# One of every 128 gathers of the first layer moved from GpSimd to SyncE, as one-row transfers

## The reference, cut to what matters

```python
def _L0_gnn_ref(node_features, edge_features, edge_index, We1, be1, We2, be2, Wn1, bn1, Wn2, bn2):
    src_f = node_features[src]
    dst_f = node_features[dst]
    edge_in = jnp.concatenate([src_f, dst_f, edge_features], axis=1)
    h = jax.nn.relu(edge_in @ We1 + be1)
    edge_msg = jax.nn.relu(h @ We2 + be2)
    node_in = jnp.concatenate([dst_f, edge_msg], axis=1)
    h2 = jax.nn.relu(node_in @ Wn1 + bn1)
    node_msg = jax.nn.relu(h2 @ Wn2 + bn2)
    agg = jax.ops.segment_sum(node_msg, dst, num_segments=node_features.shape[0])
    return node_features + agg

h = jnp.maximum(_layernorm(x, axis=-1), 0.0)
x = x + _L0_gnn_ref(h, edge_attr_64, edge_index, ...)
h = jnp.maximum(_layernorm(x, axis=-1), 0.0)
x = x + _L1_gnn_ref(h, src, dst, edge_type_8, edge_weight1, ...)   # H[etype, src] summed over dst
```

## Time and profile before

| what | value |
|---|---|
| median of three runs | 11777.57 us |
| the profiled execution, its own time | 11662.24 us |
| its span in the profile | 11659.8 us |
| PE busy | 7838.2 us, 67% |
| POOL busy | 5846.3 us, 50% |
| DVE busy | 4276.2 us, 37% |
| ACT busy | 2363.0 us, 20% |
| POOL L617 from `p_tab` (first layer) | 3128 gathers, 943 ns each |
| mean granted TensorE clock | 0.78 of full speed |

### The profile page before, as it was taken

How to read it: one execution, slowest core, us unless ns; L and a number is a source line. 1 busy time by engine, 2 the same in 40 slices (tenths; PEclk the granted TensorE clock), 3 DMA queues, 4 the chain that set the end, 5 groups by cost and what they waited for, 6 DMA issues and landing times.

```text
span 11659.8 us, 215368 instructions
## 1 busy us (share of the span) xinstructions
PE 7838.2 (67%) x52954; PEld 6037.6 (52%) x52954; DVE 4276.2 (37%) x15012; ACT 2363.0 (20%) x7307; POOL 5846.3 (50%) x6213
## 2 busy tenths in 40 slices
PE   6777777777777777776555655655565555655555
PEld 5655566565665566565444444444444444444444
DVE  4333333333333333334333333333333333333333
ACT  4333333333333333334000000000000000000000
POOL 3555555555555555554444444444444444444444
PEclk8888888888888888888776777767767776777777
DMA  4222222222222222222111111111111111111111
GB/s 105 64 64 63 63 64 63 63 64 64 63 64 64 63 63 64 62 64 76 35 34 34 35 35 35 36 35 34 35 35 34 35 35 34 36 35 35 35 35 52
DMA packets 630303, 585.31 MB, mean 50 GB/s; under 512 B 306227, under 2 KB 505147, under 8 KB 629228
## 3 DMA queue, kind: packets, MB, share of 16 engines
q0 software_dynamic: 197856, 251.86, 9.9%
q1 hardware_dynamic: 422268, 325.27, 9.7%
q10 hardware_dynamic: 9600, 1.60, 0.1%
HBM read 558.88 MB, written 19.27 MB: 50 GB/s over the span
## 4 chain that ended last, share of the span: by engine, by line
SPq 31%; issue 21%; DVE 0%; PE 0%; DMA 0%; ACT 0%; DVEq 0%
SPq L548 26%; SPq L543 4%; SPq L448 1%; SPq L538 0%; SPq L555 0%; DVE res L1057 0%; SPq L414 0%; SPq L354 0%; PE bank L1222 0%; PE bank L1209 0%; DMA h_tab<-h_place 0%; PE bank L1255 0%; SPq L564 0%; DMA h_place<-in_src_t 0%; ACT h_place L660 0%
## 5 line engine op out<-in xcount | busy, mean ns | idle before, releaser
L617 POOL DMA_INDIRECT rows_place<-h_tab,idx x3055 | 2881.8, 943 | 3237.7 <-DMA idx<-in_src_t 1871.4
L617 POOL DMA_INDIRECT shared<-p_tab,idx x3128 | 2950.0, 943 | 2472.7 <-remote 992.1
L1209 PE MATMUL bank<-shared,rows_place 128*128 128x256 f32 x6110 | 2155.8, 508 | 902.4 <-DMA rows_place<-h_tab,idx 609.7
L1021 DVE SCALAR_TENSOR_TENSOR shared<-bank,key,late 128x256 f32<-128x256 f32 x3128 | 1280.3, 476 | 2932.8 <-remote 1843.2
L1209 PEld LDWEIGHTS bank<-shared,rows_place 128*128 128x128 f32 x6110 | 1490.7, 255 | 1286.0 <-DMA rows_place<-h_tab,idx 629.1
L1115 PE MATMUL bank<-h_sb,w_tile 128*128 128x128 f32 x6256 | 1079.3, 325 | 892.8 <-DVE h_sb L932 874.4
L1115 PEld LDWEIGHTS bank<-h_sb,w_tile 128*128 128x128 f32 x6256 | 909.8, 224 | 1105.0 <-DVE h_sb L932 1095.1
L775 ACT ACTIVATE h_place<-bank 128x256 f32<-128x256 f32 x782 | 298.7, 383 | 5773.2 <-remote 3342.2
L1222 PE MATMUL bank<-h_place,w_rel_sb 128*128 128x64 f32 x6256 | 915.2, 297 | 332.1 <-issue 331.4
L1134 PE MATMUL bank<-wn_half,h_sb 128*128 128x128 f32 x6256 | 1078.3, 326 | 0.0
L1222 PEld LDWEIGHTS bank<-h_place,w_rel_sb 128*128 128x128 f32 x6256 | 844.1, 212 | 348.6 <-issue 323.3
(11 more groups left out here) (94 smaller groups left out, 7034.4 us busy)
## 6 DMA issues: line engine op xcount, KB each, us to landing
rows_place<-in_dst_c SPq DMA_DIRECT2D x782, 192.0 KB
h_place<-h_tab SPq DMA_DIRECT2D x6272, 0.5 KB
shared<-in_edge_cols SPq DMA_DIRECT2D x782, 128.0 KB
shared<-p_tab,idx POOLq DMA_INDIRECT x3128
h_place<-h_tab ACTq DMA_DIRECT2D x3072, 0.5 KB
rows_place<-h_tab,idx POOLq DMA_INDIRECT x3055
qr_f<-qr_tab SPq DMA_DIRECT2D x782, 36.0 KB
idx<-in_src_t SPq DMA_DIRECT2D x393, 8.0 KB, 1.7
```

Of the source, the lines that this page charges most:

```text
L617: pool.indirect_dma_start(out=rows_of[s][:, t, :], out_offset=None, in_=table, in_offset=bass.IndirectOffsetOnAxis(ap=idx[k][:, s * TC + t ...
L1021: ins = dve.scalar_tensor_tensor(out=hot_rel[u % 2][:, t, :], in0=ps_key, scalar=key[k][:, n * TC + t:n * TC + t + 1], in1=w_f[:, ds(c.i * ...
L1209: pe.matmul(bank[s][:, 0:RW], there, hot_rel[s % 2][:, t, :], start=(t == 0), stop=(t == TC - 1))
```

## The change

With LONG = 32, NLONG = 24, PIECE = 4 and PAST = 3, the chunks 31, 63, ... 767 of the first layer (the last of each 32, 24 chunks, all in slot 3) have three tiles gathered by POOL. Their tile 0 is fetched by SP into a buffer of its own, `fed_p`: at the first chunk of each 32 the 128 source numbers are loaded into `fed_p_ids` (L539), and from the fourth on SP reads four of them into registers behind each chunk's loads (one TENSOR_LOAD, L546) and issues four loads of one 128-byte row each (L551). At three of the 29 chunks it does this twice, which makes the 32 pieces. PE takes the chunk's rows by four matmuls of one tile each (L1160) instead of one of all four (L1163).

Besides this SP reads the first nodes of four chunks by one TENSOR_LOAD at slot 0 (L523), loads source numbers at slot 2 instead of slot 3, behind a wait for the gathers of slot 0 (L470), and the load of the second set of numbers ahead of the layer goes. SP and POOL now run the first layer in a loop of 32 chunks (L361), 24 times, and PE in one of 32 chunks (`pipelined_long`, L404); ACT and DVE keep theirs of 4.

```diff
+    LONG = 2 * SUP
+    NLONG = NCH // LONG
+    PIECE = 4
+    PAST = 3
...
+        fed_p = sb("fed_p", [P, H1])
+        fed_p_ids = sb("fed_p_ids", [1, P], i32)
...
+        def is_fed_p(i):
+            return i % LONG == LONG - 1 and i // LONG < NLONG
+
+        def pieces_fed_at(i):
+
+            extra = [10 + 7 * k for k in range(P // PIECE - (LONG - PAST))]
+            first = i - PAST + sum(e < i for e in extra)
+            return range(first, first + 1 + (i in extra))
+
+        def pipelined_long(m_, eng, step):
...
+            step(at(0), None, None, fed(0))
+            step(at(1), at(0), None, fed(1))
+            with eng.Fori(0, NLONG) as long:
+                for i in range(2, LONG + 2):
+                    step(*(at(k, long) for k in (i, i - 1, i - 2)), fed(i, long))
...
                     sp.dma_start(dst_wide[s], dst_c[ds(c.i, 1), :].rearrange("c e -> (c e)").partition_broadcast(3 * W))\
                       .then_inc(dst_wide_landed[s], 16)
-                    if s == SL - 1 and later:
+                    if s == 0:
+                        _, starts[:] = nc.values_load_multi_w_load_instructions(
+                            base_i[0:1, ds(c.i, SL)], engines=(sp.engine,), min_val=0, max_val=TOP,
+                            skip_runtime_bounds_check_because="VectorE clips a window's first node to 0 and TOP")
+                    if s == 2 and not (after is None and u > NCH - NSUP * SUP - SL):
+                        sp.wait_ge(prow_landed[0], 16 * TC * c.turn + 16 * TC)
+                        hold(sp)
                         load_idx(c.quad + 1, 1 - k, idx_landed)
-                    start = window_start(sp, c)
                     sp.wait_ge(split_hi[s], c.turn + 1)
                     hold(sp)
-                    sp.dma_start(qr_f[s][:, :], qr_tab[ds(start, W), :]...
+                    sp.dma_start(qr_f[s][:, :], qr_tab[ds(starts[s], W), :]...
                       .then_inc(qr_landed[s], 16)
...
+                def feed_p(i, turn, long):
+                    if i == 0:
+                        sp.dma_start(fed_p_ids[0:1, :], src_t[:, ds((long * LONG + LONG - 1) * TC, 1)].rearrange("p o -> o p"),
+                                     allow_slow_non_contiguous=True).then_inc(fed_p_ids_landed, 16)
+                    if i == PAST:
+                        sp.wait_ge(fed_p_ids_landed, 16 * turn + 16)
+                        hold(sp)
+                    if i >= PAST:
+                        for piece in pieces_fed_at(i):
+                            _, at = nc.values_load_multi_w_load_instructions(
+                                fed_p_ids[0:1, piece * PIECE:(piece + 1) * PIECE], engines=(sp.engine,), ...)
+                            for k, row in enumerate(at):
+                                p = piece * PIECE + k
+                                sp.dma_start(fed_p[p:p + 1, :], p_tab[ds(row, 1), :]).then_inc(fed_p_landed, 16)
...
+            def step0(c, u, k, two, lone, after):
+                fed = after and is_fed_p(lone.half * SUP + u)
+                gather(c, k, two, p_tab, prow, h1_summed, idx_landed, prow_landed, range(1 if fed else 0, TC))
...
-                pe.wait_ge(prow_landed[s], 16 * TC * c.turn + 16 * TC)
-                pe.matmul(ps_h1[:, 0:P], prow[s][:, :, :].rearrange("p t o -> p (t o)"), ident[:, :], start=False, stop=True)\
-                  .then_inc(h1_summed[s], 1)
+                pe.wait_ge(prow_landed[s], 16 * tiles_gathered_last if s == SL - 1 else 16 * TC * c.turn + 16 * TC)
+                if fed:
+                    pe.wait_ge(fed_p_landed, 16 * P * tiles_fed)
+                    for t in range(TC):
+                        ins = pe.matmul(ps_h1[t * H1:(t + 1) * H1, 0:P], prow[s][:, t, :] if t else fed_p[:, :], ident[:, :],
+                                        start=False, stop=True)
+                else:
+                    ins = pe.matmul(ps_h1[:, 0:P], prow[s][:, :, :].rearrange("p t o -> p (t o)"), ident[:, :], start=False, stop=True)
+                ins.then_inc(h1_summed[s], 1)
```

More of the change, by code:

```diff
@@ L375, in tiles_gathered @@
                     + (TC * (u // SL + 1) - (u >= FED_AT)))
[L377 to L388, removed]
+        assert NLONG == NSUP // 2 and NCH - NLONG * LONG < LONG and P // PIECE - (LONG - PAST) in range(4)
+        def is_fed_p(i):
[5 more added lines that the diff above has]
+        def pipelined_long(m_, eng, step):
+            at = lambda i, long=0: Chunk(m_, long * (LONG // SL) + i // SL, i % SL)
+            past = lambda i: min((i + 1) // LONG, NLONG)
+            fed = lambda i, long=0: (is_fed_p(i), m_ * NLONG + long + past(i),
+                                     m_ * (TC * SLOT_USES[SL - 1] - NLONG) + long * (TC * LONG // SL - 1) + TC * (i // SL + 1) - past(i))
+            step(at(0), None, None, fed(0))
[3 more added lines that the diff above has]
+                    step(*(at(k, long) for k in (i, i - 1, i - 2)), fed(i, long))
+            for i in range(2 + LONG * NLONG, NCH):
+                step(at(i), at(i - 1), at(i - 2), fed(i))
+            step(None, at(NCH - 1), at(NCH - 2), None)
+            step(None, None, at(NCH - 1), None)
         def pipelined(m_, eng, step):
@@ L488, in layer0_pass, with step @@
                 hold(sp)
-                def step(c, k, later):
+                starts = []
+                def step(c, u, k, two, lone, after):
                     s = c.slot
@@ L500, in step @@
                         load_idx(c.quad + 1, 1 - k, idx_landed)
-                    start = window_start(sp, c)
                     sp.wait_ge(split_hi[s], c.turn + 1)
                     hold(sp)
-                    sp.dma_start(qr_f[s][:, :], qr_tab[ds(start, W), :].rearrange("(a w) o -> a w o", a=1).broadcast_to([3, W, QR]))\
+                    sp.dma_start(qr_f[s][:, :], qr_tab[ds(starts[s], W), :].rearrange("(a w) o -> a w o", a=1).broadcast_to([3, W, QR]))\
                       .then_inc(qr_landed[s], 16)
-                quads_after_first(sp, m, step)
+                    if after:
+                        feed_p(lone.half * SUP + u, m * NLONG + lone.two, lone.two)
@@ L508, in layer0_pass @@
+                superchunks(sp, m, step)
                 for s in range(SL):
@@ L1152, in _, with step @@
             passes = number_of_passes(pe)
-            def step(c, before, before2, after, after2, after3):
+            def step(c, before, before2, fed):
                 if before:
@@ L1158, in step @@
                 if c:
-                    sum_h1(c)
+                    sum_h1(c, *fed)
                 if before2:
```

16 lines of the change are left out of this document (8 added, 8 removed).

## The result

The changed kernel takes 11943.79 us, the median of four runs (11937.74 to 11963.97), beside 11781.43 us before (11773.84 to 11794.78): 1.014 times, 95% interval 1.0125 to 1.0155. It is slower by 162 us, where 10 us less were forecast.

A forecast was written before the change was run, and what follows sets the result against it. In the first layer no engine is full; gathers pace 0.70 of chunks, PE the rest. Terms -21 - 9 + 13 + 5 + 2 + 0 = -10 us, 11652 of 11662 profiled, forecast as 11768; range 11722 to 11855.

The forecast's parts named there:

- SP's term: SP's register reads and row loads in the first layer fit beside its other work: 0 us, bounds 0 and +160.
- Rival 3: SP becomes the bound, edge columns and `qr_f` come late and PE waits: 7.04 us a chunk, 11928 us; chance 0.12.
- The sum: SP's rows, register reads, other loads and ids added up: 172 us of the 219 that 32 chunks last, 5.4 a chunk.
- Gathers less: POOL does one gather less in 24 chunks, 1.25 us gained in 0.70 of them: -21 us, bounds 0 and -30.
- PE's branch: PE's 24 long-loop branches of 3.48 us stay hidden by a 0.2 us margin: +5 us, bounds 0 and +84.
- rival 2: PE's branch stall delays the next post by up to 3.27 us in 24 rounds: 11829 us, slower; chance 0.12.
- POOL's release: POOL's 32-chunk loop starts gathers 0 to 0.05 us later in 0.70 of 782 chunks: +13 us, bounds 0 and +27.
- Rival 4: Posts or POOL's wake come 0.05 to 0.1 us later in all chunks, using up the gathers' gain: 11811 us; chance 0.08.
- The pauses: POOL's pauses after each 104 gathers now wander and cost less in 17 cases: -9 us, bounds -21 and +9.

The follow-up runs named there:

- long_64: Changed kernel with one tile of every 64 chunks fed, two rows a piece, loops of 64 chunks, whole result: 11923.79 us, 1.0125 times before, first kind of chip.
- no_feed: Changed kernel without SP's ids load, register reads and row loads, POOL still spared 24 gathers: 7895.03 us, 0.9958 times before, quicker chip.
- loops_only: Changed kernel without SP's feeding, with all four gathers and one matmul again: 7925.08 us, 0.9998 times before, quicker chip.
- after_again: The changed kernel itself, unchanged, timed on the quicker kind of chip: 8265.21 us, 1.0413 times before.
- rows_and_gathers: Changed kernel with POOL gathering all four tiles in every chunk while SP fetches the rows too: 8266.16 us, 1.043 times before, quicker chip.
- reads_no_rows_3: Changed kernel without row loads (register reads also gone from the built program), POOL spared 24 gathers: 11826.60 us, 1.0029 times before, first kind of chip.
- long_48: Changed kernel with one tile of every 48 chunks fed, loops of 48 chunks, whole result: 11833.50 us, 1.0048 times before, first kind of chip.

## Why the prediction was wrong

**The step that failed is SP's term**, "the undisturbed value is the nearer one, and I take 0, bounds 0 and +160". It measured near its upper bound. On the first kind of chip the changed kernel is +162 us and the version without rows +31.5 us, so rows and their register reads cost 130 us; on the quicker chip, 8265 against 7907 us in one set, 358 us. Rival 3 had the mechanism and nearly the size (11928 for 11944 measured), with a chance of 0.12, and the range left it out. Its signs are there: SP's waits are gone, and `qr_f` comes late.

Two things made the choice wrong. First the price of a row. I reasoned that rows cost 0.98 us in the second layer because of long rows of gathers there, and that four gathers would not do it. But POOL was busy 552 of 1000 us in the first layer, more than enough for the rows to stand beside gathers: four took 2.6 us on the mean, against 1.5 undisturbed. The value measured beside running gathers was the one to carry over. Second the register read: 0.80 us for four numbers, not 0.6. The Trainium skill's 200 ns a register ("Runtime: NRT & Kernel Launch", section "Instruction fetch mechanics"), which I set aside, gives 0.8 us for four, and here the trace agrees, though not for eight (1.04 us), two (0.98, in long_64) or one (0.43).

At 7.1 us a chunk SP is over the 6.53 us of a chunk paced by gathers and over the mean of 6.83. The sum had 5.4. On the quicker chip 5.4 is what SP took, but as a sum of other parts, and that is luck: 2.3 us of loads where the sum had 3.0 to 3.1, 1.1 from there to the first row where it had 0.6 for the read, and 0.5 behind the last row where it had nothing. The gaps around the read and behind the rows are not in the sum, and they are there on both kinds of chip.

**Gathers less: right for the chunk, lost in the sum.** A chunk with three gathers takes 5.25 to 5.7 us at full clock, 5.28 forecast; in the changed kernel:

```profile
1456.77 0.35 DVE L981 TENSOR_SCALAR h_sb<-bank,be_col 128x128 f32<-128x128 f32 x1 [3.05 <-remote]
...
1462.22 0.35 DVE L981 TENSOR_SCALAR h_sb<-bank,be_col 128x128 f32<-128x128 f32 x1 [1.81 <-PE bank L1163]
```

The worth of a gather is shown by no_feed against loops_only, where 24 are 30 us. With SP over the pace it goes: after_again and rows_and_gathers, 24 gathers apart, are within 11 us. On the first kind of chip it wasn't measured alone.

**PE's branch (rival 2): hidden less than thought.** It takes 3.7 us, where the earlier trace rows had 3.48. In reads_no_rows_3, the 23 chunks in which it takes over 1 us last 7.54 us on the mean by DVE's timeline, all chunks 6.94: about 0.6 us each, 14 us in all in place of 5. In the changed kernel they last 8.10 us against 7.12, about 1 us each. Rival 2 needed 2 us to make the result slower. On the quicker chip loops_only is equal to before.

**POOL's release: right.** The gathers start 0.80 us after a post in the changed kernel (median of the held chunks; 0.77 before), within the 0 to 0.05 us allowed. In reads_no_rows_3, with the same loop and no rows, it is 0.77 again, so the 0.02 us go with the rows and not with POOL's loop.

**Rival 4, small costs alone,** has a share. Without rows the kernel is 31.5 us slower on the first kind of chip (1.0019 to 1.0039, the gain of 24 gathers within), and 30 us quicker on the other. PE's branch makes 14 us of it. If the gathers gave back the 21 us forecast, 31.5 + 21 - 14 = some 40 us are left for the loops, the base read and the moved load; no run parts these.

**The pauses** can't be judged in the changed kernel, where SP is over the pace. In reads_no_rows_3, where it isn't, 14 early posts come behind the third gather, and the two chunks take 13.9 us in the median, near the 13.7 forecast. The price before was read too low: the prediction had 14.33 us from one pair, and the median of the 17 pairs in that trace is 15.08.

## What to carry to other kernels

Before work is given to an idle queue, add up its step at the price that its instructions have beside what will run at the same time, and take the dearer row where both stand in the trace. An engine that waits half of its time has only that half to give, and past it the excess is paid in every round: on the quicker chip 0.4 us in each of 782 chunks. Here SP's work rose by some 3.7 us a chunk (a step of 7.12 us less the 3.38 us for which it was busy before) where 3.45 were free, and a gain of 1.25 us in one chunk of 32 can't pay for that.

## What the runs showed of the hardware

The same program has two paces by chip, 7926 us and 11776 us, with the granted clock at 0.94 and 0.79. In the slow one, a post by PE is seen only 1.1 to 1.5 us after POOL's last gather in a row (in the earlier trace rows L1108 had ended 1.9 us earlier), and SP's one-row issues, 0.44 us apart on the mean otherwise, are 0.98 us apart within a row of gathers. In the quick one neither happens. A register read of four numbers took 802 ns on both, of eight 1035 ns, of two 978 ns in long_64: the time does not follow their number alone. No version with the whole result beats the kernel before on the first kind of chip. On the quicker one the half-fed kernel (0.996) keeps the gathers' gain while SP has time left, but half of its rows are left out, and neither long_48 nor long_64 was timed there.
